# GNN layer on one core: transposing transfers in place of TensorE's transposes of h

## Chip, cores and metric

One core of a Trainium2 chip runs the whole layer. The metric is the device time of one execution in microseconds (us). The kernel before took 1001.66 us (median of three runs, 1001.43 to 1001.74).

## What is computed

x is 8192 x 256 (fp32), adj is 8192 x 8192 (int32, 0 or 1). Cut to what matters:

```
h    = relu(layernorm(x))                        # rows of x, eps 1e-5
self = h @ W_self + b_self
agg  = (adj > 0) @ h / max(degree, 1)
nb   = agg @ W_nb + b_nb
out  = x + relu(concat(self, nb) @ W_comb + b_comb)
```

## The kernel before

The weights are multiplied together first, so that one product of h with 512 columns gives a self part (256 columns, kept in fp32 as `self_f`) and a part z (256 columns) that the adjacency then sums. The kernel has two stages.

The **projection stage** makes z and the self part. The 8192 rows are 64 tiles of 128 rows, taken in 32 pairs (`PAIRS`), and x comes in 16 chunks (`CHUNKS`) of four tiles, 512 KB each, so a chunk is two pairs. For each pair j the engines do this:

- VectorE (`dve`): `stats_of(j)` (lines 432 to 442), the mean and variance of its rows, two BATCH_NORM_STATS2 and two aggregates.
- GpSimd (`pool`, lines 251 to 260): once for each chunk, four small instructions turn mean and variance into a scale and a shift. They wait until VectorE has aggregated all four tiles of the chunk (line 252).
- ScalarE (`act`): `norm(j)` (line 264) writes h = relu(scale x + shift) over x in `self_f`.
- TensorE (`pe`): `turn(j)` (line 326), four fp32 transposes into one bank of PSUM (`turn_ps`).
- ScalarE: `high_of_h(j)` (line 272) copies the turned h to fp16. VectorE: `low_of_h(j)` (line 444) subtracts that copy from the turned h and writes the remainder as fp16. High and low half of h stand in a ring of three slots (`h_t`, RING = 3).
- TensorE: `project(j)` (line 339), 12 matmuls of 512 columns into a pair of banks (`pair_ps`, a ring of three): for each of two tiles and two halves of the inner dimension, high times high, high times low and low times high.
- ScalarE: `copy_self(j)` and `high_of_z(j)` empty the bank, VectorE: `low_of_z(j)` writes the low half of z.

Each engine's order is written out by hand. On VectorE step j of the loop at line 514 is low_of_h(j + 1), low_of_z(j - 2), stats_of(j + 6), and in the four steps of `MASK_STEPS` one mask of the first adjacency tile (`form_mask`, `turn_mask`). On TensorE it is turn(j + 2), project(j). SyncE (`sp`) issues every transfer: first all 16 chunks of x with the first adjacency tile's four groups (1 MB each) between them, then tiles 1 and 2 of the adjacency, one group at a time as mask buffers come free (`load_tile`, line 182).

The **summing stage** goes over 64 tiles of the adjacency's rows: VectorE makes a 0/1 mask and transposes it in blocks, ScalarE counts it, TensorE multiplies it with z in 64 matmuls (`sum_chunk`, line 355), and VectorE finishes the tile. `tile(0, 0)` on TensorE begins as soon as the last projection is out.

Of the kernel before, what the change touches and what calls it, by code (L numbers as in the profile page):

```python
# [5 lines left out]
F32 = mybir.dt.float32  # L6
# [35 lines left out]
RING = 3  # L42

MASK_STEPS = (5, 11, 17, 23)

# [3 lines left out]
def graph_layer(nc, x, adj, w_self_t, w_nb_t, w_comb, b_cols_in, b_comb, out):  # L49
# [6 lines left out]
    with ExitStack() as ctx:  # L56
# [3 lines left out]
        def sem(name):  # L60
            return ctx.enter_context(nc.semaphore(name))
# [23 lines left out]
        PAIR = 2 * 2 * HALVES * P  # L85
        h_t = spare[:, 0:RING * PAIR].rearrange("p (n i t h m) -> p n i t h m", n=RING, i=2, t=2, h=HALVES)
        w12 = spare[:, RING * PAIR:RING * PAIR + 4 * HALVES * D].rearrange("p (i h n) -> p i h n", i=2, h=HALVES)

# [31 lines left out]

        turn_ps = [ctx.enter_context(nc.psum_tensor(f"turn_ps{n}", [P, 2 * D], F32)) for n in range(2)]
        pair_ps = [ctx.enter_context(nc.psum_tensor(f"pair_ps{n}", [P, 2, 2 * D], F32)) for n in range(RING)]

        acc = [pair_ps[2][:, 0, :], pair_ps[2][:, 1, :], pair_ps[0][:, 0, :], pair_ps[0][:, 1, :]]
        deg_ps = [turn_ps[0][:, 0:1], turn_ps[1][:, 0:1], pair_ps[1][:, 0, 0:1], pair_ps[1][:, 1, 0:1]]

# [20 lines left out]
        normed = sem("normed")  # L147
        h_turned = sem("h_turned")
        h_high = sem("h_high")
# [25 lines left out]
        def _(sp):  # L175
# [11 lines left out]
            def store(r):  # L187
                sp.wait_ge(out_ready, r + 1)
                sp.dma_start(out[r, :, :], x_again[:, r % XRING, :]).then_inc(stored, DONE)

            load_x(0)
            for n, (dst, w) in enumerate(((ws_t, w_self_t), (wn_t, w_nb_t))):
# [6 lines left out]
            sp.dma_start(bc_row, b_comb.rearrange("(a n) -> a n", a=1).partition_broadcast(P)).then_inc(b_loaded, DONE)  # L199
            for e in range(2, 6):  # L200
                load_x(e)
            for a in range(QUAD):
                load_group(0, a)
                load_x(6 + a)
            for e in range(6 + QUAD, CHUNKS):
                load_x(e)
            for r in range(1, 3):
# [33 lines left out]
        @block.gpsimd  # L241
        def _(pool):
            pool.memset(ident, 0.0).then_inc(zeroed, 1)
            pool.memset(power, -0.5).then_inc(zeroed, 1)
            pool.memset(ones, 1.0).then_inc(zeroed, 1)
            pool.memset(eight[:, :], SUM_HELD).then_inc(zeroed, 1)
            pool.wait_ge(zeroed, 4)
            pool.affine_select(out=ident, in_=ident, compare_op=ALU.not_equal, fill=1.0, base=0,
                               pattern=[[-1, P]], channel_multiplier=1).then_inc(ident_ready, 1)

            for e in range(CHUNKS):
                pool.wait_ge(aggr_done, SUB * (e + 1))
                pool.tensor_scalar(var_s[:, e % 2, :], mean_var[:, e, :, 1], EPS, H_SCALE ** -2,
                                   ALU.add, ALU.mult).then_inc(var_ready, 1)
                pool.tensor_scalar(minus_mean[:, e % 2, :], mean_var[:, e, :, 0], -1.0, None, ALU.mult).then_inc(negated, 1)
                pool.wait_ge(var_ready, e + 1)
                pool.tensor_tensor(rstd[:, e, :], var_s[:, e % 2, :], power, ALU.pow).then_inc(rstd_ready, 1)
                pool.wait_ge(rstd_ready, e + 1)
                pool.wait_ge(negated, e + 1)
                pool.tensor_tensor(shift[:, e, :], minus_mean[:, e % 2, :], rstd[:, e, :], ALU.mult).then_inc(shift_ready, 1)  # L260

        @block.scalar
        def _(act):
# [7 lines left out]

            def high_of_h(j):
                act.wait_ge(h_turned, j + 1)
                if j >= RING:
                    act.wait_ge(projected, j - RING + 1)
                act.activation(h_t[:, j % RING, 0, :, :, :].rearrange("p t h m -> p (t h m)"), turn_ps[j % 2][:, :],  # L276
                               ACT.Copy).then_inc(h_high, 1)

            def high_of_z(j):
                act.activation(z16[:, 2 * j:2 * j + 2, 0:D], pair_ps[j % RING][:, :, D:2 * D], ACT.Copy, scale=Z_SCALE  # L280
                               ).then_inc(z_high, 1)

            def copy_self(j):
                act.wait_ge(projected, j + 1)
                act.activation(self_f[:, 2 * j:2 * j + 2, :], pair_ps[j % RING][:, :, 0:D], ACT.Copy, scale=SELF_SCALE  # L285
                               ).then_inc(self_copied, 1)
# [8 lines left out]
            for n in range(2):  # L295
# [3 lines left out]
                               ).then_inc(w_high, 1)  # L299
            high_of_h(0)  # L300
            norm(2)

            for j in range(PAIRS + 1):
                if j + 1 < PAIRS:
                    high_of_h(j + 1)
                if j + 3 < PAIRS:
                    norm(j + 3)
                if j >= 1:
                    copy_self(j - 1)
                    high_of_z(j - 1)  # L310
                for a, at in enumerate(COUNT_STEPS):
                    if at == j:
                        count(0, 0, a)
# [11 lines left out]
        def _(pe):  # L325
            def turn(j):
                pe.wait_ge(normed, 2 * (j + 1))
                if j >= 2:
                    pe.wait_ge(h_low, j - 1)
                for t in range(2):  # L330
                    for half in range(HALVES):
                        at = (t * HALVES + half) * P
                        mm = pe.transpose(turn_ps[j % 2][:, at:at + P], self_f[:, 2 * j + t, half * P:(half + 1) * P],  # L333
                                          ident)
                mm.then_inc(h_turned, 1)

            TERMS = ((0, 0), (0, 1), (1, 0))

            def project(j):
                pe.wait_ge(h_low, j + 1)  # L340
                if j == 0:
                    pe.wait_ge(w_ready, 2)
                if j >= RING:
                    pe.wait_ge(z_low, j - RING + 1)
                    pe.wait_ge(self_copied, j - RING + 1)
                if j == 2:
                    pe.wait_ge(c_ready, 1)
                for t in range(2):
                    steps = [(half, i, w) for half in range(HALVES) for i, w in TERMS]
                    for at, (half, i, w) in enumerate(steps):  # L350
                        mm = pe.matmul(pair_ps[j % RING][:, t, :], h_t[:, j % RING, i, t, half, :], w12[:, w, half, :],  # L351
                                       start=(at == 0), stop=(at == len(steps) - 1))
                mm.then_inc(projected, 1)
# [14 lines left out]

            pe.wait_ge(ident_ready, 1)
            for n, w_t in enumerate((ws_t, wn_t)):  # L370
# [5 lines left out]
                mm.then_inc(w_product, 1)  # L376
            turn(0)
            turn(1)
            pe.wait_ge(wide_ready, 2 * HALVES)
# [4 lines left out]
            for j in range(PAIRS):  # L384
                if j + 2 < PAIRS:
                    turn(j + 2)
                project(j)
# [30 lines left out]
        def _(dve):  # L418
# [25 lines left out]
            def low_of_h(j):  # L444
                flat = "p t h m -> p (t h m)"
                dve.wait_ge(h_high, j + 1)
                dve.scalar_tensor_tensor(h_t[:, j % RING, 1, :, :, :].rearrange(flat), turn_ps[j % 2][:, :], 1.0,  # L447
                                         h_t[:, j % RING, 0, :, :, :].rearrange(flat), ALU.mult, ALU.subtract
                                         ).then_inc(h_low, 1)

            def low_of_z(j):
                dve.wait_ge(z_high, j + 1)
                dve.scalar_tensor_tensor(z16[:, 2 * j:2 * j + 2, D:2 * D], pair_ps[j % RING][:, :, D:2 * D], Z_SCALE,  # L453
                                         z16[:, 2 * j:2 * j + 2, 0:D], ALU.mult, ALU.subtract).then_inc(z_low, 1)
# [52 lines left out]
            w_low(1)  # L507
            low_of_h(0)
            for p in range(4, 6):
                stats_of(p)  # L510
# [3 lines left out]
            for j in range(PAIRS + 2):  # L514
                if j + 1 < PAIRS:
                    low_of_h(j + 1)
                if j >= 2:
                    low_of_z(j - 2)
                if j + 6 < PAIRS:
                    stats_of(j + 6)  # L520
                if j in MASK_STEPS:
                    a = MASK_STEPS.index(j)
                    form_mask(0, a, first=True)
                    turn_mask(0, 0, a)
# [69 lines left out]
```

## Time and profile before

| | |
|---|---|
| median of three runs | 1001.66 us |
| the profiled execution | 1001.76 us, of which its span is 1000.0 us |
| projection stage, TensorE (first projection to first sum) | 14.96 to 110.50 us of the span |
| summing stage, TensorE | 110.50 us to 996.3 us |
| granted clock of TensorE over the span | 1.0 |

The span runs from the first to the last instruction in the trace; the rest of the execution's time (1.76 us) lies around it. In the rows below an instruction is named by its engine and its line in the kernel (L351 is line 351), by what it writes and reads, and by its shape. PE is TensorE's matmuls, PEld its weight loads, DVE is VectorE, ACT ScalarE, POOL GpSimd, SP SyncE. A tensor that lies inside another bears the other's name: h_t and the product of the weights lie in `mask_t`, the statistics in `x_again`, h and x in `self_f`.

### The profile page before, as it was taken

How to read it: one execution, taken by the hardware profiler on the slowest of the kernel's cores; microseconds unless marked ns; L12 is line 12 of the kernel's file. 1: busy time of each engine (PE TensorE's matmuls, PEld its weight loads, DVE VectorE, ACT ScalarE, POOL GpSimd, SP SyncE). 2: the span in 40 equal slices, each digit the busy share in tenths (PEclk: the TensorE clock that was granted, in tenths of full speed). 3: DMA queues.
4: the chain of work that ended last, by engine and by line, in shares of the span. 5: the costliest groups of instructions: out<-in, count | busy, mean ns of one | idle time of the engine just before them, and what ended most of it. 6: DMA issues, size and time to landing. Idle time of an engine off the chain costs nothing.

```text
span 1000.0 us, 14269 instructions
## 1 busy us (share of the span) xinstructions
PE 989.9 (99%) x4696; PEld 460.5 (46%) x4696; DVE 673.9 (67%) x1163; ACT 585.0 (59%) x675; POOL 30.5 (3%) x73
## 2 busy tenths in 40 slices
PE   7999999999999999999999999999999999999998
PEld 4555444444444444444444444444444444444443
DVE  6886677986776666766667666676666766667711
ACT  5888886775655556655556555565555655556500
POOL 2332000000000000000000000000000000000000
PEclk9999999999999999999999999999999999999999
DMA  9621399999888898888988888888888888888600
GB/s 344 251 85 43 140 421 371 416 420 377 320 316 321 312 341 317 319 322 312 342 312 322 322 313 336 318 322 322 312 328 328 323 315 321 321 326 326 218 16 10
DMA packets 58994, 295.04 MB, mean 295 GB/s; under 512 B 6624, under 2 KB 24160, under 8 KB 26208
## 3 DMA queue, kind: packets, MB, share of 16 engines
q1 hardware_dynamic: 58976, 294.81, 78.6%
q8 instruction: 10, 0.16, 0.1%
q14 instruction: 8, 0.07, 0.0%
HBM read 286.39 MB, written 8.39 MB: 295 GB/s over the span
## 4 chain that ended last, share of the span: by engine, by line
PE 98%; DMA 1%; DVE 0%; SPq 0%; issue 0%
PE pair_ps L360 89%; PE pair_ps L351 8%; PE turn_ps L333 1%; DMA self_f<-in_x_dram 1%; PE pair_ps L381 0%; DVE x_again L439 0%; SPq L195 0%; SPq L193 0%; DVE z L505 0%; DVE fold L502 0%; DVE x_again L442 0%; DVE part L485 0%; DVE part L482 0%; DVE x_again L488 0%; SPq L177 0%
## 5 line engine op out<-in xcount | busy, mean ns | idle before, releaser
L360 PE MATMUL pair_ps<-z,mask_t 128*128 128x512 f16 x4096 | 885.8, 379 | 0.0
L290 ACT ACTIVATE mask<-mask 128x2048 uint8<-128x2048 uint8 x256 | 488.0, 1908 | 341.4 <-DVE mask_t L430 341.4
L360 PEld LDWEIGHTS pair_ps<-z,mask_t 128*128 128x128 fp8e4 x4096 | 396.2, 98 | 475.7
L430 DVE STREAM_TRANSPOSE mask_t<-mask 128x512 uint32<-128x512 uint32 x256 | 181.7, 710 | 219.8 <-PE pair_ps L360 214.3
L424 DVE TENSOR_SCALAR mask<-stage 128x2048 uint8<-128x2048 int32 x256 | 308.1, 1203 | 6.0 <-DMA stage<-in_adj_dram 5.9
L351 PE MATMUL pair_ps<-mask_t 128*128 128x512 f16 x384 | 87.8, 379 | 0.0
L351 PEld LDWEIGHTS pair_ps<-mask_t 128*128 128x128 f16 x384 | 37.6, 98 | 38.6
L290 ACT ACTIVATION_READ_ACCUMULATOR mask<-mask 128x1 f32 x256 | 48.1, 188 | 0.0
L482 DVE SCALAR_TENSOR_TENSOR part<-pair_ps,rdeg,self_f 128x256 f32<-128x256 f32 x64 | 31.0, 484 | 15.7 <-DVE rdeg L477 11.9
L269 ACT ACTIVATE self_f<-self_f,x_again 128x256 f32<-128x256 f32 x64 | 35.0, 605 | 8.7 <-POOL x_again L260 8.7
L447 DVE SCALAR_TENSOR_TENSOR mask_t<-turn_ps,mask_t 128x512 f16<-128x512 f32 x32 | 21.8, 681 | 19.3 <-ACT mask_t L276 19.3
L485 DVE SCALAR_TENSOR_TENSOR part<-pair_ps,rdeg,part 128x256 f32<-128x256 f32 x64 | 31.0, 484 | 2.3
L488 DVE SCALAR_TENSOR_TENSOR x_again<-part,x_again 128x256 f32<-128x256 f32 x64 | 27.2, 425 | 2.2
L439 DVE BATCH_NORM_STATS2 x_again<-self_f 128x6 f32<-128x256 f32 x64 | 23.7, 411 | 7.3 <-DMA self_f<-in_x_dram 7.3
L285 ACT ACTIVATE self_f<-pair_ps 128x512 f32<-128x512 f32 x32 | 19.1, 597 | 14.8 <-PE pair_ps L351 14.8
L453 DVE SCALAR_TENSOR_TENSOR z<-pair_ps,z 128x512 f16<-128x512 f32 x32 | 21.8, 681 | 5.6 <-ACT z L280 5.6
L470 DVE TENSOR_TENSOR self_f<-self_f,c_row 128x256 f32 (+1 forms) x64 | 24.5, 383 | 0.0
L276 ACT ACTIVATE mask_t<-turn_ps 128x512 f16<-128x512 f32 x32 | 19.3, 603 | 0.0
L461 DVE SCALAR_TENSOR_TENSOR spread<-deg_part,fold 128x128 f16<-128x128 f32 x64 | 18.0, 281 | 1.8 <-ACT mask L290 1.8
L333 PE MATMUL turn_ps<-x_again,self_f 128*128 128x128 f32 x128 | 19.1, 273 | 0.0
L280 ACT ACTIVATE z<-pair_ps 128x512 f16<-128x512 f32 x32 | 19.0, 594 | 0.0
L333 PEld LDWEIGHTS turn_ps<-x_again,self_f 128*128 128x128 f32 x128 | 15.9, 141 | 6.0 <-ACT self_f L269 0.3
(31 smaller groups left out, 93.0 us busy)
## 6 DMA issues: line engine op xcount, KB each, us to landing
stage<-in_adj_dram SPq DMA_DIRECT2D x256, 1024.0 KB, 5.9
self_f<-in_x_dram SPq DMA_DIRECT2D x16, 512.0 KB, 15.4
x_again<-in_x_dram SPq DMA_DIRECT2D x64, 128.0 KB, 5.3
out_dram<-x_again SPq DMA_DIRECT2D x64, 128.0 KB, 5.1
z<-in_L_gnn_W_comb_dram SPq DMA_DIRECT2D x2, 256.0 KB, 4.8
z<-in_L_gnn_W_self_dram SPq DMA_DIRECT2D x1, 256.0 KB, 3.6
z<-in_L_gnn_W_nb_dram SPq DMA_DIRECT2D x1, 256.0 KB, 4.5
z<-in_L_gnn_b_comb_dram SPq DMA_DIRECT2D x1, 128.0 KB, 6.4
```

What stands on the lines that cost most here:

```text
L269: act.activation(t, t, ACT.Relu, bias=shift[:, e, s:s + 1], scale=rstd[:, e, s:s + 1]).then_inc(normed, 1)
L290: act.activation(mask[:, a, :], mask[:, a, :], ACT.Copy, accum_out=deg_part[:, n, a:a + 1]).then_inc(counted, 1)
L333: mm = pe.transpose(turn_ps[j % 2][:, at:at + P], self_f[:, 2 * j + t, half * P:(half + 1) * P], ident)
L351: mm = pe.matmul(pair_ps[j % RING][:, t, :], h_t[:, j % RING, i, t, half, :], w12[:, w, half, :], start=(at == 0), stop=(at == len(steps) ...
L360: mm = pe.matmul(acc[n], bytes_of[:, :, s], z16[:, SUB * e + s, :], start=(e == 0 and s == 0), stop=(e == CHUNKS - 1 and s == SUB - 1))
L424: dve.tensor_scalar(mask[:, a, :], stage[:, a, :], 0.0, float(ONE_BYTE), ALU.is_gt, ALU.mult).then_inc(masked, 1)
L430: dve.transpose(mask_t[:, n, :, a, :], src).then_inc(transposed, 1)
L439: dve.bn_stats(stats[:, e % 2, s, :], self_f[:, SUB * e + s, :]).then_inc(stats_done, 1)
L470: dve.tensor_tensor(own_of(r), own_of(r), c_row[:, :], ALU.add).then_inc(biased, 1)
L482: dve.scalar_tensor_tensor(part[:, :], acc[n][:, D:2 * D], rdeg[:, n:n + 1], own, ALU.mult, ALU.add).then_inc(low_added, 1)
L485: dve.scalar_tensor_tensor(part[:, :], acc[n][:, 0:D], rdeg[:, n:n + 1], part[:, :], ALU.mult, ALU.add).then_inc(sum_read, 1)
L488: dve.scalar_tensor_tensor(x_again[:, n, :], part[:, :], 0.0, x_again[:, n, :], ALU.max, ALU.add).then_inc(out_ready, 1)
```

## The change

- h is no longer turned by TensorE. GpSimd casts h (`self_f`, rows as they are) to fp16, `high_of_h(j)`, one instruction of 128 x 512 for each pair; VectorE's `low_of_h(j)` subtracts it from h, both read from SBUF; both halves go to a new ring `h16` of three slots. SyncE then issues two transposing transfers for each pair (`turn(j)`, one for each tile, 128 rows x 512 columns of fp16, from `h16` to `h_t`), and `project(j)` waits for these.
- ScalarE's `high_of_h` and TensorE's `turn` are gone, and so are the two banks `turn_ps`: `pair_ps` has four pairs of banks (`BANKS`) in place of three.
- GpSimd's work for a chunk becomes `rstd_of(e)` and its order is: chunks 0 and 1, then for each pair j the cast, and after every odd pair the chunk (j + 3) / 2.
- VectorE's loop does low_of_h(j + 2) at step j, ScalarE's does norm(j + 4).
- SyncE issues chunks 0 to 3 of x at the start, and then, pair by pair, one chunk at every even pair (chunk j / 2 + 4), one group of the first adjacency tile at pairs 1, 7, 13 and 19, and `turn(j)`, which waits for low_of_h(j) and, from pair 3 on, for project(j - 3). Tiles 1 and 2 of the adjacency follow after turn(31).

The diff, cut to its core:

```diff
+BANKS = 4
+
+LOAD_STEPS = (1, 7, 13, 19)
 MASK_STEPS = (5, 11, 17, 23)
...
+        h16 = spare[:, 0:RING * PAIR].rearrange("p (n t i d) -> p n t i d", n=RING, t=2, i=2)
+        h_t = spare[:, RING * PAIR:W_AT].rearrange("p (n t i h m) -> p n t i h m", n=RING, t=2, i=2, h=HALVES)
...
+            def turn(j):
+                sp.wait_ge(h_low, j + 1)
+                if j >= RING:
+                    sp.wait_ge(projected, j - RING + 1)
+                    sp.wait_ge(h_turned[j % RING], 2 * (j // RING) * DONE)
+                for t in range(2):
+                    sp.dma_start_transpose(h_t[:, j % RING, t, :, :, :].rearrange("p i h m -> p (i h) m"),
+                                           h16[:, j % RING, t, :, :].rearrange("p i d -> p (i d)")
+                                           ).then_inc(h_turned[j % RING], DONE)
...
-            for e in range(2, 6):
-                load_x(e)
-            for a in range(QUAD):
-                load_group(0, a)
-                load_x(6 + a)
-            for e in range(6 + QUAD, CHUNKS):
-                load_x(e)
+            load_x(2)
+            load_x(3)
+            for j in range(PAIRS):
+                e = j // 2 + 4
+                if j % 2 == 0 and e < CHUNKS:
+                    load_x(e)
+                if j in LOAD_STEPS:
+                    load_group(0, LOAD_STEPS.index(j))
+                turn(j)
             for r in range(1, 3):
                 load_tile(r)
...
-            for e in range(CHUNKS):
+            def rstd_of(e):
                 pool.wait_ge(aggr_done, SUB * (e + 1))
...
+            def high_of_h(j):
+                pool.wait_ge(normed, 2 * (j + 1))
+                if j >= RING:
+                    pool.wait_ge(h_turned[j % RING], 2 * (j // RING) * DONE)
+                pool.tensor_copy(h16[:, j % RING, :, 0, :], self_f[:, 2 * j:2 * j + 2, :]).then_inc(h_high, 1)
+
+
+            rstd_of(0)
+            rstd_of(1)
+            for j in range(PAIRS):
+                high_of_h(j)
+                if j % 2 and (j + 3) // 2 < CHUNKS:
+                    rstd_of((j + 3) // 2)
...
             def project(j):
-                pe.wait_ge(h_low, j + 1)
+                pe.wait_ge(h_turned[j % RING], 2 * (j // RING + 1) * DONE)
...
-                if j >= RING:
-                    pe.wait_ge(z_low, j - RING + 1)
-                    pe.wait_ge(self_copied, j - RING + 1)
+                if j >= BANKS:
+                    pe.wait_ge(z_low, j - BANKS + 1)
+                    pe.wait_ge(self_copied, j - BANKS + 1)
...
             for j in range(PAIRS):
-                if j + 2 < PAIRS:
-                    turn(j + 2)
                 project(j)
...
             def low_of_h(j):
-                flat = "p t h m -> p (t h m)"
                 dve.wait_ge(h_high, j + 1)
-                dve.scalar_tensor_tensor(h_t[:, j % RING, 1, :, :, :].rearrange(flat), turn_ps[j % 2][:, :], 1.0,
-                                         h_t[:, j % RING, 0, :, :, :].rearrange(flat), ALU.mult, ALU.subtract
-                                         ).then_inc(h_low, 1)
+                dve.scalar_tensor_tensor(h16[:, j % RING, :, 1, :], self_f[:, 2 * j:2 * j + 2, :], 1.0,
+                                         h16[:, j % RING, :, 0, :], ALU.mult, ALU.subtract).then_inc(h_low, 1)
...
             low_of_h(0)
+            low_of_h(1)
             for p in range(4, 6):
                 stats_of(p)
...
             for j in range(PAIRS + 2):
-                if j + 1 < PAIRS:
-                    low_of_h(j + 1)
+                if j + 2 < PAIRS:
+                    low_of_h(j + 2)
                 if j >= 2:
                     low_of_z(j - 2)
                 if j + 6 < PAIRS:
                     stats_of(j + 6)
```

## Rows read from the trace of the kernel before

**Rows 1.** The page: busy time by engine, and the last-ending chain by line.

```profile
PE 989.9 (99%) x4696; PEld 460.5 (46%) x4696; DVE 673.9 (67%) x1163; ACT 585.0 (59%) x675; POOL 30.5 (3%) x73
...
PE pair_ps L360 89%; PE pair_ps L351 8%; PE turn_ps L333 1%; DMA self_f<-in_x_dram 1%; PE pair_ps L381 0%; DVE x_again L439 0%; SPq L195 0%; SPq L193 0%; DVE z L505 0%; DVE fold L502 0%; DVE x_again L442 0%; DVE part L485 0%; DVE part L482 0%; DVE x_again L488 0%; SPq L177 0%
```

**Rows 2.** Both stages: busy us (instructions) by engine; last: clock, DMA share, GB/s.

```profile
14.85:110.29 95.44, 95.44 (x503) 51.17 (x502) 71.47 (x182) 78.68 (x153) 26.32 (x56) 1.00 0.37 144
110.29:996.00 885.71, 885.71 (x4162) 402.42 (x4160) 593.71 (x950) 499.71 (x512) 0.00 (x0) 1.00 0.83 313
```

**Rows 3.** Timeline: start and duration in us; [idle before, releaser]. Projection's first and last.

```profile
14.96 2.75 PE L351 MATMUL pair_ps<-mask_t 128*128 128x512 f16 x12
...
110.50 38.15 PE L360 MATMUL pair_ps<-z,mask_t 128*128 128x512 f16 x176
```

**Rows 4.** Timeline, one step of a pair: TensorE and VectorE.

```profile
32.45 0.66 DVE L447 SCALAR_TENSOR_TENSOR mask_t<-turn_ps,mask_t 128x512 f16<-128x512 f32 x1
...
32.68 0.60 PE L333 MATMUL turn_ps<-x_again,self_f 128*128 128x128 f32 x4
...
33.02 0.68 DVE L453 SCALAR_TENSOR_TENSOR z<-pair_ps,z 128x512 f16<-128x512 f32 x1
33.12 2.75 PE L351 MATMUL pair_ps<-mask_t 128*128 128x512 f16 x12
...
33.62 0.73 DVE L439 BATCH_NORM_STATS2 x_again<-self_f 128x6 f32<-128x256 f32 x2
...
34.39 0.25 DVE L442 BATCH_NORM_AGGREGATE x_again<-x_again 128x2 f32<-128x6 f32 x2
34.55 0.66 DVE L447 SCALAR_TENSOR_TENSOR mask_t<-turn_ps,mask_t 128x512 f16<-128x512 f32 x1
...
35.71 0.60 PE L333 MATMUL turn_ps<-x_again,self_f 128*128 128x128 f32 x4
```

**Rows 5.** Timeline, GpSimd's work for one chunk, and what released it.

```profile
25.10 0.25 DVE L442 BATCH_NORM_AGGREGATE x_again<-x_again 128x2 f32<-128x6 f32 x2
...
25.44 0.19 POOL L253 TENSOR_SCALAR x_again<-x_again 128x4 f32<-128x4 f32 x1 [3.99 <-DVE x_again L442]
...
27.02 0.20 POOL L260 TENSOR_TENSOR x_again<-x_again 128x4 f32<-128x4 f32 x1
```

**Rows 6.** Timeline, GpSimd's larger instructions at the start.

```profile
0.73 0.20 POOL L243 MEMSET x_again<- 128x128 f32 x1 [0.29 <-POOLq L572]
...
0.87 0.10 POOL L244 MEMSET x_again<- 128x4 f32 x1
...
1.38 0.29 POOL L248 TENSOR_SCALAR_AFFINE_SELECT x_again<-x_again 128x128 f32<-128x128 f32 x1 [0.24 <-POOL eight L246]
```

**Rows 7.** The page's groups: VectorE's three-input forms, count, busy us, mean ns.

```profile
L482 DVE SCALAR_TENSOR_TENSOR part<-pair_ps,rdeg,self_f 128x256 f32<-128x256 f32 x64 | 31.0, 484 | 15.7 <-DVE rdeg L477 11.9
...
L488 DVE SCALAR_TENSOR_TENSOR x_again<-part,x_again 128x256 f32<-128x256 f32 x64 | 27.2, 425 | 2.2
```

**Rows 8.** Timeline, a mask on VectorE and GpSimd's instruction beside it.

```profile
30.58 1.19 DVE L424 TENSOR_SCALAR mask<-stage 128x2048 uint8<-128x2048 int32 x1
30.75 1.07 POOL L253 TENSOR_SCALAR x_again<-x_again 128x4 f32<-128x4 f32 x1 [3.53 <-DVE x_again L442]
```

**Rows 9.** Timeline around chunk 1: GpSimd's last instruction, and VectorE's weights.

```profile
12.46 1.28 DVE L493 SCALAR_TENSOR_TENSOR mask_t<-pair_ps,mask_t 128x512 f16<-128x512 f32 x2
...
12.93 0.20 POOL L260 TENSOR_TENSOR x_again<-x_again 128x4 f32<-128x4 f32 x1
```

**Rows 10.** SyncE's issue of one transfer (timeline), and x's landing times (tile view).

```profile
10.66 0.44 SPq L177 DMA_DIRECT2D self_f<-in_x_dram  x1
...
DMA to landing us min/median/max: 3.4/15.4/21.2
```

**Rows 11.** Timeline, the second adjacency tile's first mask.

```profile
113.30 1.22 DVE L424 TENSOR_SCALAR mask<-stage 128x2048 uint8<-128x2048 int32 x1
```

More of the change, by code:

```diff
@@ L85, in graph_layer @@
         PAIR = 2 * 2 * HALVES * P
-        h_t = spare[:, 0:RING * PAIR].rearrange("p (n i t h m) -> p n i t h m", n=RING, i=2, t=2, h=HALVES)
-        w12 = spare[:, RING * PAIR:RING * PAIR + 4 * HALVES * D].rearrange("p (i h n) -> p i h n", i=2, h=HALVES)
+        W_AT = 2 * RING * PAIR
+        h16 = spare[:, 0:RING * PAIR].rearrange("p (n t i d) -> p n t i d", n=RING, t=2, i=2)
+        h_t = spare[:, RING * PAIR:W_AT].rearrange("p (n t i h m) -> p n t i h m", n=RING, t=2, i=2, h=HALVES)
+        w12 = spare[:, W_AT:W_AT + 4 * HALVES * D].rearrange("p (i h n) -> p i h n", i=2, h=HALVES)
         late = z16[:, 3 * TILES // 4:, :].rearrange("p t n -> p (t n)").bitcast(F32)
@@ L119, in graph_layer @@
         power = small(SUB)
[L121 to L125, printed above, removed]
+        pair_ps = [ctx.enter_context(nc.psum_tensor(f"pair_ps{n}", [P, 2, 2 * D], F32)) for n in range(BANKS)]
+        acc = [pair_ps[0][:, 0, :], pair_ps[0][:, 1, :], pair_ps[1][:, 0, :], pair_ps[1][:, 1, :]]
+        deg_ps = [pair_ps[2][:, 0, 0:1], pair_ps[2][:, 1, 0:1], pair_ps[3][:, 0, 0:1], pair_ps[3][:, 1, 0:1]]
         w_loaded = [sem(f"w_loaded{n}") for n in range(2)]
@@ L147, in graph_layer @@
         normed = sem("normed")
-        h_turned = sem("h_turned")
+        h_turned = [sem(f"h_turned{n}") for n in range(RING)]
         h_high = sem("h_high")
@@ L270, in norm @@
                                    ).then_inc(normed, 1)
-            def high_of_h(j):
-                act.wait_ge(h_turned, j + 1)
-                if j >= RING:
-                    act.wait_ge(projected, j - RING + 1)
-                act.activation(h_t[:, j % RING, 0, :, :, :].rearrange("p t h m -> p (t h m)"), turn_ps[j % 2][:, :],
-                               ACT.Copy).then_inc(h_high, 1)
             def high_of_z(j):
-                act.activation(z16[:, 2 * j:2 * j + 2, 0:D], pair_ps[j % RING][:, :, D:2 * D], ACT.Copy, scale=Z_SCALE
+                act.activation(z16[:, 2 * j:2 * j + 2, 0:D], pair_ps[j % BANKS][:, :, D:2 * D], ACT.Copy, scale=Z_SCALE
                                ).then_inc(z_high, 1)
@@ L284, in copy_self @@
                 act.wait_ge(projected, j + 1)
-                act.activation(self_f[:, 2 * j:2 * j + 2, :], pair_ps[j % RING][:, :, 0:D], ACT.Copy, scale=SELF_SCALE
+                act.activation(self_f[:, 2 * j:2 * j + 2, :], pair_ps[j % BANKS][:, :, 0:D], ACT.Copy, scale=SELF_SCALE
                                ).then_inc(self_copied, 1)
@@ L299, in _ @@
                                ).then_inc(w_high, 1)
-            high_of_h(0)
             norm(2)
+            norm(3)
             for j in range(PAIRS + 1):
-                if j + 1 < PAIRS:
-                    high_of_h(j + 1)
-                if j + 3 < PAIRS:
-                    norm(j + 3)
+                if j + 4 < PAIRS:
+                    norm(j + 4)
                 if j >= 1:
@@ L325, in _ @@
         def _(pe):
[L326 to L335, printed above, removed]
             TERMS = ((0, 0), (0, 1), (1, 0))
             def project(j):
-                pe.wait_ge(h_low, j + 1)
+                pe.wait_ge(h_turned[j % RING], 2 * (j // RING + 1) * DONE)
                 if j == 0:
                     pe.wait_ge(w_ready, 2)
-                if j >= RING:
-                    pe.wait_ge(z_low, j - RING + 1)
-                    pe.wait_ge(self_copied, j - RING + 1)
+                if j >= BANKS:
+                    pe.wait_ge(z_low, j - BANKS + 1)
+                    pe.wait_ge(self_copied, j - BANKS + 1)
                 if j == 2:
@@ L350, in project @@
                     for at, (half, i, w) in enumerate(steps):
-                        mm = pe.matmul(pair_ps[j % RING][:, t, :], h_t[:, j % RING, i, t, half, :], w12[:, w, half, :],
+                        mm = pe.matmul(pair_ps[j % BANKS][:, t, :], h_t[:, j % RING, t, i, half, :], w12[:, w, half, :],
                                        start=(at == 0), stop=(at == len(steps) - 1))
@@ L367, in sum_degrees @@
                           start=True, stop=True).then_inc(deg_summed, 1)
-            pe.wait_ge(ident_ready, 1)
             for n, w_t in enumerate((ws_t, wn_t)):
@@ L376, in _ @@
                 mm.then_inc(w_product, 1)
-            turn(0)
-            turn(1)
             pe.wait_ge(wide_ready, 2 * HALVES)
@@ L444, in low_of_h @@
             def low_of_h(j):
-                flat = "p t h m -> p (t h m)"
                 dve.wait_ge(h_high, j + 1)
-                dve.scalar_tensor_tensor(h_t[:, j % RING, 1, :, :, :].rearrange(flat), turn_ps[j % 2][:, :], 1.0,
-                                         h_t[:, j % RING, 0, :, :, :].rearrange(flat), ALU.mult, ALU.subtract
-                                         ).then_inc(h_low, 1)
+                dve.scalar_tensor_tensor(h16[:, j % RING, :, 1, :], self_f[:, 2 * j:2 * j + 2, :], 1.0,
+                                         h16[:, j % RING, :, 0, :], ALU.mult, ALU.subtract).then_inc(h_low, 1)
             def low_of_z(j):
                 dve.wait_ge(z_high, j + 1)
-                dve.scalar_tensor_tensor(z16[:, 2 * j:2 * j + 2, D:2 * D], pair_ps[j % RING][:, :, D:2 * D], Z_SCALE,
+                dve.scalar_tensor_tensor(z16[:, 2 * j:2 * j + 2, D:2 * D], pair_ps[j % BANKS][:, :, D:2 * D], Z_SCALE,
                                          z16[:, 2 * j:2 * j + 2, 0:D], ALU.mult, ALU.subtract).then_inc(z_low, 1)
@@ L514, in _ @@
             for j in range(PAIRS + 2):
-                if j + 1 < PAIRS:
-                    low_of_h(j + 1)
+                if j + 2 < PAIRS:
+                    low_of_h(j + 2)
                 if j >= 2:
```

## The prediction

> **What bounds the kernel now.** I read the profile's page first. TensorE is busy 99% of the span and the chain that ended last is nearly all TensorE: sums 89%, projections 8%, transposes 1% [rows 1]. So time is won only by TensorE doing less before its last sum, and lost by any gap opened in it. The view by stretches then splits the span [rows 2]: 95.44 us of projection stage and 885.7 us of summing stage, TensorE without a gap in both, clock 1.00. The change touches the first alone. The sums have 13.84 us a tile (885.7 / 64), and their first instruction comes at 110.50 [rows 3]: whatever moves that moment moves the end by as much.
>
> The timeline of one pair shows what that stage costs [rows 4]. From one transpose group to the next are 35.71 - 32.68 = 3.03 us: 0.44 for the transposes (32.68 to 33.12) and 2.59 for the 12 matmuls (33.12 to 35.71). VectorE's step of low_of_h, low_of_z and statistics is 34.55 - 32.45 = 2.10 us, so it has slack. GpSimd works 1.78 us for a chunk (25.44 to 27.22) and otherwise waits, always for VectorE's aggregates [rows 5].
>
> **The change, part by part.** *Removed from TensorE:* 30 of the 32 transpose groups lie in the stretch, 30 x 0.44 = 13.2 us, all on the path. Kept fed, TensorE would need 32 x 2.59 = 82.9 us.
>
> *GpSimd's order.* This decides, in my reading of the code. The work for chunk (j + 3) / 2 stands behind the cast of odd pair j and waits for the statistics of pair j + 4. VectorE takes these in step j - 2, behind low_of_h(j), which waits for that very cast. And the cast of pair j + 1 stands behind the chunk's work on GpSimd, while VectorE's next instruction, low_of_h(j + 1), waits for it. So the two engines take turns, once for every chunk (two pairs). One round, from rows:
> - aggregate to GpSimd: 25.35 to 25.44, 0.09;
> - the chunk's four instructions, 1.78;
> - the cast of the even pair: c;
> - back to VectorE: 0.09, taken alike;
> - VectorE's step of the even pair: 2.10 (the odd pair's cast runs beside it);
> - VectorE's step of the odd pair to the end of its aggregates: 32.45 to 34.64, 2.19.
>
> Together 6.25 + c.
>
> *The cast c* (512 elements, fp32 to fp16) is not in the trace. GpSimd's memsets take 0.10 for 4 elements and 0.20 for 128 [rows 6]; 0.83 ns an element gives 0.10 + 508 x 0.00083 = 0.53, the low end, since a memset reads nothing. The select takes 0.29 for 128; on the same base that is 1.5 ns an element and 0.89 us, and four times 0.29 is 1.17, the high end. I take 0.89, since the select reads and writes as a cast does. The round is then **7.14 us, 3.57 a pair, against 3.03 before**.
>
> *low_of_h* now reads h from SBUF. The same form from PSUM takes 484 ns and from SBUF 425 for 256 columns [rows 7]; I leave it at its 0.66, and count 0.06 a piece, 0.12 a round, for the low end. At the high end it is blocked (rival 1).
>
> *Masks.* In four steps a mask follows the statistics, and GpSimd's first instruction beside it took 1.07 in place of 0.19 [rows 5, 8]. That is off the path now and on it then: 4 x 0.88 = 3.5. The mask itself (30.58 to 32.45, where low_of_h starts [rows 4, 8]) is hidden behind GpSimd's 1.78 + 0.88 + c.
>
> *The start.* GpSimd finishes chunk 1 at 13.13 and VectorE the weights at 13.74 [rows 9]; the casts of pairs 0 and 1 end at 14.91. low_of_h(1) and two steps of statistics (0.09 + 0.57 + 0.93 + 1.02) bring the last aggregate to 17.52. The first round has no low_of_z (2 x 0.60 less): 17.61 + 5.94 = 23.55. Twelve rounds of 7.14 follow: 109.2, with the masks 112.7. There chunk 15 begins; 1.78 + 0.89 + 0.09 + 0.66 later low_of_h(28) is done: 116.1.
>
> *The transfers.* Two a pair, issued by SyncE. A transposing transfer is not in the trace. An issue takes 0.44, and the quickest chunk of x (four times the bytes) landed 3.4 us after its issue [rows 10]: 0.44 + 3.4 = 3.8 from low_of_h to project. Pair 28 starts at 119.9. From there TensorE is fed, since a transfer may take the 5.2 us that two projections last. The low end is a quarter of 3.4, 3 us less; the high end is two landings one after the other, 7.2 a pair (rival 2).
>
> *End:* 119.9 + 4 x 2.59 = 130.3, against 110.50: **+19.8 us**. On the execution's own 1001.76 that is 1021.6; the median lies 0.10 below it, which I neglect. I give 1022.
>
> *Costed at nothing.* ScalarE loses 32 casts, but it is no bound: 78.68 busy of 95.44 [rows 2]. The fourth pair of banks lets TensorE run further ahead, of no use to one that starves. The chunks of x, moved between the steps, are issued eight pairs before their rows are turned, some 28 us. If this cover is gone VectorE's statistics wait for x and the round is longer by that. SyncE's issues are 0.88 a pair, 0.22 for x, four groups, all below 3.57. Tile 1's adjacency, issued so far as its stage buffers came free, now stands behind turn(31), which waits for project(28): at about 123.4 it is issued; the first group lands 3.4 later, at the 313 GB/s of the summing stage [rows 2] a megabyte takes 3.3, so the fourth lands near 137 and its mask stands near 139, due by 130.3 + 13.84 = 144. Before, VectorE formed the first of these masks 2.8 us after the sums began [rows 3, 11]; it is hidden with some 5 us to spare.
>
> **The rivals.** *1. The cast holds VectorE up.* GpSimd goes straight from the even pair's cast to the odd pair's, just when low_of_h of the even pair should start. That a GpSimd instruction can be held through one of VectorE's is in the rows: the 1.07 above ended at 31.82, with the mask that ended at 31.77 [rows 8]. If low_of_h waits for the odd cast in this way, the round grows by c: 14 times 0.89, +12.5, **1034**. Against: that row has a mask, not this form, and GpSimd as the one that waits; were low_of_h first, the cast would wait, which costs nothing. The Trainium skill (SBUF — State Buffer, "Who interferes with whom") says that a VectorE instruction with two SBUF inputs and a GpSimd instruction that reads SBUF exclude each other, the first to start holding the ports to its end. By that, low_of_h as it is now written comes under the rule, and the sum would be 1034 where the cast starts first and 1022 where it does not.
>
> *2. The transfers bound.* Over 3.57 a pair the queue decides in place of the round, each 0.1 us adding 3.2. Nothing in the trace tells a transposing transfer's pace; between 0.88 and 7.2 a pair lies 3.57, and at 4.5 the stage ends near 14.9 + 32 x 4.5 + 4 = 163, **1054**. Against: 3.4 is mostly delay, which overlaps from transfer to transfer. The Trainium skill (VectorE: DVE Perf Modes, "The three transpose paths") gives 1309 ns for a 128 x 128 block by DMA. Eight such blocks a pair, if they ran one by one, would be an estimated 10.5 us and a time near 1240; no row here bears on it.
>
> *3. TensorE stays fed, and the change wins.* Place: the round. It decides at two pairs of the old pace: were the round about 5.7 us or less, 14 times 1.4 would take the 19.8 back. At 5.2 (2 x 2.59) TensorE is the bound: first projection at 14.0 + 0.7 + 3.8 = 18.5, end 18.5 + 82.9 = 101.4, 9.1 earlier, **993**. For: TensorE loses 0.44 a pair. Against: with c at its low end the round is still 6.78, and 6.25 with no cast at all; only a chunk's work shorter than its 1.78, which no edit shortens, would do it.
>
> *4. No change:* a round near 5.7, needing the same and a chance meeting.
>
> **How the numbers follow.** Chances: forecast 0.52, cast holding VectorE 0.27, transfers 0.13, faster 0.05, no change 0.03. A measurement of this kernel can tell 0.2%, 2 us, from no change. Slower is 0.52 + 0.27 + 0.13 = 0.92. Range: the low end of the cast, 16 casts x 0.36 = 5.8 less, and low_of_h's 1.6 less, give 1014, and a quicker landing a little under: 1013. The high end, 16 x 0.28 = 4.5 more, gives 1026, and rival 1 with it 1034 to 1042; I stop at 1038. Left out are most of rival 2 and rivals 3 and 4, about 2 in 10.
>
> **What would show it.** In the changed kernel's trace the first sum should begin near 130, not 110. TensorE should have gaps in the projection stage, about 2 us in every two pairs, ended by the transfers. GpSimd's L253 should wait for VectorE's aggregate once per chunk, and VectorE's low_of_h of even pairs for GpSimd's cast, for some 2.7 us; the starts of GpSimd's chunk work should stand 7.1 us apart. Cast: 0.53 to 1.17. If low_of_h of even pairs starts only when the odd cast ends, or lasts 1.5 us, rival 1 holds. If SyncE's issues stand end to end, or VectorE has long waited when transfers land, rival 2. The forecast is wrong if chunk starts follow TensorE's pace (5.2 or 6.1 apart), or if a wait for x or adjacency opens gaps in the summing stage.

## The result, and the profile after

The changed kernel takes **1022.4 us** (median of 4 runs) against 1001.7: a ratio of 1.0205, 95% interval 1.019 to 1.022. The forecast was 1022, range 1013 to 1038. Ratios here and below compare the executions that agree with one another; two of the ten of experiment 9, at 2694.69 and 3710.02 us, are left out of its ratio, and no trace shows what made them slow.

Lines of the page after: busy time, the chain that ended last by line, and three groups that answer to [rows 1, 5, 7].

```profile
PE 984.6 (96%) x4568; PEld 445.9 (44%) x4568; DVE 679.0 (67%) x1163; ACT 569.1 (56%) x643; POOL 48.4 (5%) x105
...
PE pair_ps L370 87%; DVE x_again L444 2%; PE pair_ps L361 2%; DVE z L456 1%; DVE mask_t L451 1%; POOL mask_t L282 1%; DVE x_again L447 1%; PE pair_ps L383 1%; POOL x_again L269 1%; DMA z<-in_L_gnn_W_comb_dram 0%; DMA mask_t<-mask_t 0%; POOL x_again L271 0%; POOL x_again L276 0%; SPq L201 0%; POOL x_again L273 0%
...
L451 DVE SCALAR_TENSOR_TENSOR mask_t<-self_f,mask_t 128x512 f16<-128x512 f32 x32 | 26.8, 839 | 30.8 <-POOL mask_t L282 30.8
...
L282 POOL CAST mask_t<-self_f 128x512 f16<-128x512 f32 x32 | 18.8, 611 | 5.0 <-DMA mask_t<-mask_t 5.0
...
mask_t<-mask_t SPq DMA_TRANSPOSE x64, 2.6
```

TensorE is busy 5 us less, yet its share falls to 96%: the chain no longer runs through its projections (8% before, 2% now) but through VectorE and GpSimd. The stretches of the two stages (columns as in [rows 2]) place the loss.

```profile
18.67:130.20 111.53, 89.78 (x381) 36.93 (x382) 73.69 (x173) 61.91 (x121) 41.86 (x84) 0.95 0.70 169
130.20:1016.10 885.90, 885.90 (x4163) 402.46 (x4162) 594.39 (x951) 500.69 (x512) 0.00 (x0) 1.00 0.84 316
```

The first stretch, which ends 0.84 us before the first sum, has 22 us of gaps in TensorE's work (111.53 less 89.78 busy); before there were none. The timeline has the first sum at 131.04, against 110.50 in [rows 3]: 20.5 us later, which is all of the 20.5 by which the span grew. From the first sum to the end of the span it is 889.5 us in both (1020.5 less 131.04, 1000.0 less 110.50): the summing stage is what it was.

```profile
131.04 4.26 PE L370 MATMUL pair_ps<-z,mask_t 128*128 128x512 f16 x19
```

One round of GpSimd and VectorE, from the timeline after (start and duration in us):

```profile
52.24 0.25 DVE L447 BATCH_NORM_AGGREGATE x_again<-x_again 128x2 f32<-128x6 f32 x2
52.58 0.20 POOL L269 TENSOR_SCALAR x_again<-x_again 128x4 f32<-128x4 f32 x1 [4.29 <-DVE x_again L447]
...
54.31 1.17 POOL L282 CAST mask_t<-self_f 128x512 f16<-128x512 f32 x2
...
54.95 1.07 DVE L451 SCALAR_TENSOR_TENSOR mask_t<-self_f,mask_t 128x512 f16<-128x512 f32 x1 [2.46 <-POOL mask_t L282]
...
57.48 0.66 DVE L451 SCALAR_TENSOR_TENSOR mask_t<-self_f,mask_t 128x512 f16<-128x512 f32 x1
...
59.44 0.25 DVE L447 BATCH_NORM_AGGREGATE x_again<-x_again 128x2 f32<-128x6 f32 x2
...
59.77 1.07 POOL L269 TENSOR_SCALAR x_again<-x_again 128x4 f32<-128x4 f32 x1 [4.29 <-DVE x_again L447]
...
67.84 0.19 POOL L269 TENSOR_SCALAR x_again<-x_again 128x4 f32<-128x4 f32 x1 [4.29 <-DVE x_again L447]
```

GpSimd stands 4.29 us until VectorE's aggregates, VectorE 2.46 us until GpSimd's cast: each waits while the other works. From 52.58 to 59.77 are 7.19 us for two pairs. Where a mask falls in (59.77, 1.07 in place of 0.20) the round that begins there is 0.88 longer (67.84 - 59.77 = 8.07). The two casts take 0.61 each, and low_of_h of the even pair 1.07, where that of the odd pair takes 0.66.

SyncE's transposing transfers in the whole changed kernel, by line: issue in ns and landing in us (from the start of the issue to the arrival of the data), each as least, median and most; behind the issue the starts of the first and the last.

```profile
L201 SPq DMA_TRANSPOSE mask_t<-mask_t x64: 1188/1267/2398, 14.8 to 125.3; - x64
...
DMA to landing us min/median/max: 2.4/2.6/5.9
```

### The profile page after: what moved, and what is told of

Its sections match the earlier page's. It is cut to its first block, busy times and chain, and to the rows that moved or that the text cites. A ratio compares the mean times of both kernels' runs of the same rounds, so it can differ in the third digit from the quotient of the medians.

```text
span 1020.5 us, 14074 instructions
## 1 busy us (share of the span) xinstructions
PE 984.6 (96%) x4568; PEld 445.9 (44%) x4568; DVE 679.0 (67%) x1163; ACT 569.1 (56%) x643; POOL 48.4 (5%) x105
## 4 chain that ended last, share of the span: by engine, by line
PE 89%; DVE 5%; issue 3%; POOL 2%; DMA 1%; SPq 0%; ACT 0%; POOLq 0%
PE pair_ps L370 87%; DVE x_again L444 2%; PE pair_ps L361 2%; DVE z L456 1%; DVE mask_t L451 1%; POOL mask_t L282 1%; DVE x_again L447 1%; PE pair_ps L383 1%; POOL x_again L269 1%; DMA z<-in_L_gnn_W_comb_dram 0%; DMA mask_t<-mask_t 0%; POOL x_again L271 0%; POOL x_again L276 0%; SPq L201 0%; POOL x_again L273 0%
## 5 line engine op out<-in xcount | busy, mean ns | idle before, releaser
L361 PE MATMUL pair_ps<-mask_t 128*128 128x512 f16 x384 | 90.8, 395 | 25.9 <-DMA mask_t<-mask_t 25.8
L451 DVE SCALAR_TENSOR_TENSOR mask_t<-self_f,mask_t 128x512 f16<-128x512 f32 x32 | 26.8, 839 | 30.8 <-POOL mask_t L282 30.8
L478 DVE TENSOR_SCALAR deg<-pair_ps 128x1 f32<-128x1 f32 x64 | 7.9, 123 | 37.5 <-PE pair_ps L376 37.5
L282 POOL CAST mask_t<-self_f 128x512 f16<-128x512 f32 x32 | 18.8, 611 | 5.0 <-DMA mask_t<-mask_t 5.0
L273 POOL TENSOR_TENSOR x_again<-x_again 128x4 f32<-128x4 f32 x16 | 16.6, 1037 | 0.0
```

The source lines that it names most:

```text
L282: pool.tensor_copy(h16[:, j % RING, :, 0, :], self_f[:, 2 * j:2 * j + 2, :]).then_inc(h_high, 1)
L361: mm = pe.matmul(pair_ps[j % BANKS][:, t, :], h_t[:, j % RING, t, i, half, :], w12[:, w, half, :], start=(at == 0), stop=(at == len(steps) ...
L451: dve.scalar_tensor_tensor(h16[:, j % RING, :, 1, :], self_f[:, 2 * j:2 * j + 2, :], 1.0, h16[:, j % RING, :, 0, :], ALU.mult, ALU.subtrac ...
```

## The experiments

All are the changed kernel with the edits named. Each result is the median in us, then in brackets its ratio to the kernel before, with the 95% interval; the kernel before ran beside them at medians of 1001.8 to 1002.5. The time rows come from one execution, which need not be the median one.

**1. The order on GpSimd alone.**

```diff
-                if j % 2 and (j + 3) // 2 < CHUNKS:
-                    rstd_of((j + 3) // 2)
+                if j % 2 == 0 and j >= 2 and (j + 2) // 2 < CHUNKS:
+                    rstd_of((j + 2) // 2)
```

> The changed kernel with one line of GpSimd's order changed: a chunk's four instructions stand behind the cast of an even pair j (chunk (j + 2) / 2) and no longer behind the odd pair before it, so that VectorE's step of the even pair runs beside them. By the theory that the turn-taking of GpSimd and VectorE set the pace (rounds of 7.19 us for two pairs), the round falls to about 4.7 us, SyncE's issues (2 x 1.27 + 0.29 a pair, 2.9) become the bound, the first sum comes near 111 in place of 131, and the time is 1000 to 1006 us. By the rival that the transposing transfers set the pace already, nothing moves: 1020 to 1023.

Measured 1012.2 us (ratio 1.010, 1.008 to 1.012). One moved line gives back half of the loss, so the round held the changed kernel; but 1012 is neither number. SyncE's timeline shows a candidate for the next bound, in two pairs, a chunk of x and the next two pairs:

```profile
61.81 5.28 SPq L201 DMA_TRANSPOSE mask_t<-mask_t  x4
67.13 0.58 SPq L181 DMA_DIRECT2D self_f<-in_x_dram  x1
67.82 5.57 SPq L201 DMA_TRANSPOSE mask_t<-mask_t  x4
```

SyncE issues end to end: 67.82 - 61.81 = 6.0 us for two pairs, 3.0 a pair, as slow as the old kernel's 3.03. The expectation of 2.9 left out the gaps between issues. The start came late too: the first projection begins at 19.93, 5.0 later than the 14.96 of the kernel before, and from there to the first sum at 120.12 are 100.2 us, 3.13 a pair on average. That SyncE's issues alone set this pace is not shown: GpSimd's casts also wait 19.8 us for transfers, and experiment 4 takes issues away and gains nothing.

**2. The odd cast held back**, so that nothing on GpSimd runs beside low_of_h of the even pair.

```diff
                 pool.wait_ge(normed, 2 * (j + 1))
+                if j % 2:
+                    pool.wait_ge(h_low, j)
```

> The changed kernel with one wait added: GpSimd's cast of an odd pair waits until low_of_h of the even pair before it is done. By the theory that this cast holds low_of_h up (1.07 us where it stands beside the cast, 0.66 elsewhere), low_of_h of even pairs falls to 0.66, the round from 7.19 to about 6.75, and the time by 13 x 0.43, to 1016 to 1018 us. By the rival that low_of_h of even pairs is slow for a reason of its own, its 1.07 stays, and the time is 1022 or more.

Measured 1018.6 (1.016, 1.014 to 1.018). In the view by line low_of_h is 656 to 693 ns for all 32, none at 1.07, and two chunk starts stand 51.67 - 44.84 = 6.83 apart:

```profile
44.84 0.19 POOL L269 TENSOR_SCALAR x_again<-x_again 128x4 f32<-128x4 f32 x1 [3.02 <-DVE x_again L449]
...
51.67 0.20 POOL L269 TENSOR_SCALAR x_again<-x_again 128x4 f32<-128x4 f32 x1 [3.02 <-DVE x_again L449]
```

So the cast did hold low_of_h up: without it the round is 0.36 us shorter. The time fell too, though by less than expected (1018.6 lies 0.6 above the range); the rival expectation falls.

**3. x issued by ScalarE, order as changed.** Chunks 4 and 5 at the start, 6 to 15 from ScalarE's loop.

```diff
+                if j % 2 == 0 and j // 2 + 6 < CHUNKS:
+                    e = j // 2 + 6
+                    act.dma_start(chunk_of(self_f, e)..., x[e, :, :]).then_inc(x_full[e], DONE)
```

> The changed kernel with chunks 6 to 15 of x issued by ScalarE and chunks 4 and 5 at the start, so that only the transposing transfers and four adjacency groups are left between the steps on SyncE. By the theory of the round nothing moves: 1021 to 1024 us. By the rival that SyncE's queue sets the pace, the 10 issues of 0.58 us taken out of it bring some 6 us: 1016 or less.

Measured 1023.4 (1.0215, 1.020 to 1.023). Nothing moved, as the round has it: SyncE's queue did not set the changed kernel's pace.

**4. Both 1 and 3.**

> Both: the order of e1_order and x issued by ScalarE. By the theory of the round SyncE is then left with 2 x 1.27 us a pair, about as much as TensorE's 2.59, and the first sum comes near 18.7 + 32 x 2.6 + 1 = 103: 992 to 997 us, below the kernel before. By the rival that transposing transfers bound at over 2.9 us a pair whatever is issued beside them, it stays where e1_order is.

Measured 1014.8 (1.012, 1.009 to 1.015): a miss, no better than 1, as the rival had it. The view by line has SyncE's transfers land after 2.4 to 8.4 us, median 3.5 (2.6 in the changed kernel), and GpSimd's cast waits for a transfer 16 times, 33.0 us in all.

```profile
POOL mask_t L279 <- DMA mask_t<-mask_t: 33.0, 16, 5.2
...
DMA to landing us min/median/max: 2.4/3.5/8.4
```

Unloading SyncE was worth nothing here: with a ring of three slots the cast must wait when a transfer lands late.

**5. As 4, rings of five slots** (`RING = 5`, the spare space one slot of `mask_t` earlier).

> As e4_order_xact (GpSimd's order mended, x issued by ScalarE) with rings of five slots in place of three for both halves of h. Theory: with the round gone, what was left in e4_order_xact (1015) is the time from a freed slot to a landed transfer, up to 8.4 us when a load of x or adjacency is under way, against 5.2 us that two projections cover; five slots cover four projections, 10.4 us, so TensorE is fed: first sum near 104, 994 to 999 us. Rival: the transfers' own pace beside loads is the bound, more slots only move the wait, and the time stays over 1008 us.

Measured 1011.1 (1.008, 1.007 to 1.010). The cast's waits for transfers are gone, yet TensorE still waits for them, 16.8 us in 6 waits; landing is up to 10.0 us. The time is on the rival's side. Whether the slots brought anything is open, since the intervals of 4 and 5 overlap.

```profile
PE pair_ps L361 <- DMA mask_t<-mask_t: 16.8, 6, 5.1
```

**6. One transposing transfer a pair**, 128 x 1024, order as changed.

```diff
-                for t in range(2):
-                    sp.dma_start_transpose(h_t[:, j % RING, t, ...
+                sp.dma_start_transpose(h_t[:, j % RING, ...].rearrange("p t i h m -> p (t i h) m"),
+                                       h16[:, j % RING, ...].rearrange("p t i d -> p (t i d)"))
```

The counts that wait for a pair's transfers are halved with it.

> The changed kernel with one transposing transfer of 128 x 1024 for each pair in place of two of 128 x 512; all else as changed. By the theory of the round the time stays: 1020 to 1023 us. By the rival that SyncE's issue of two transfers a pair sets the pace it falls by what the issue loses. The issue itself: if its 1.27 us is a fixed part near the 0.43 of an ordinary issue and the rest goes with the columns, one of 1024 takes some 2.1 us; if it is all columns, 2.5.

Measured 1022.7 (1.020, 1.018 to 1.022): again the round holds. The issue was expected to grow with the columns and does not: 1.23 us for 1024 columns, 1.27 for 512 (medians, view by line); landing 3.1 for 2.6.

```profile
L200 SPq DMA_TRANSPOSE mask_t<-mask_t x32: 1231/1232/1871, 15.9 to 124.8; - x32
```

**7. Order, five slots, one transfer a pair**, x with SyncE.

> The changed kernel with GpSimd's order mended (as e1_order), rings of five slots, and one transposing transfer for each pair; x stays with SyncE between the steps. Theory: SyncE's work a pair falls from about 3.07 to 2.1 + 0.29 + 0.1 = 2.5, just under TensorE's 2.59, and five slots cover the landing: first sum near 105, 994 to 1000 us, below the kernel before. Rival: the pace of the transposing transfers beside loads, not their issue, held e1_order at 1012: then over 1006 us.

Measured 1006.0 (1.0035, 1.002 to 1.005): at the edge of the rival's side. SyncE now has gaps, so its issues no longer set the pace, and the cast no longer waits for a slot. The timeline shows another round:

```profile
48.70 0.54 POOL L268 TENSOR_SCALAR x_again<-x_again 128x4 f32<-128x4 f32 x1 [2.04 <-DVE x_again L446]
...
50.86 1.09 ACT L298 ACTIVATE self_f<-self_f,x_again 128x256 f32<-128x256 f32 x2 [1.98 <-POOL x_again L275]
...
52.34 0.58 ACT L302 ACTIVATE z<-pair_ps 128x512 f16<-128x512 f32 x1
...
52.95 0.69 DVE L455 SCALAR_TENSOR_TENSOR z<-pair_ps,z 128x512 f16<-128x512 f32 x1 [0.85 <-ACT z L302]
...
54.34 0.25 DVE L446 BATCH_NORM_AGGREGATE x_again<-x_again 128x2 f32<-128x6 f32 x2
...
54.68 1.07 POOL L268 TENSOR_SCALAR x_again<-x_again 128x4 f32<-128x4 f32 x1 [2.04 <-DVE x_again L446]
```

Chunk's work, norm, high_of_z behind it, low_of_z, the statistics behind that, the next chunk's work: 54.68 - 48.70 = 5.98. Experiments 8 and 9 cut this round in two ways.

**8. As 7, statistics ahead of low_of_z** in VectorE's step.

```diff
-                if j >= 2:
-                    low_of_z(j - 2)
                 if j + 6 < PAIRS:
                     stats_of(j + 6)
+                if j >= 2:
+                    low_of_z(j - 2)
```

> As e7_order_ring_merge, but VectorE takes the statistics before low_of_z in each step. Theory: what held e7_order_ring_merge at 6.0 us for two pairs is a second, longer round: chunk's work on GpSimd, norm on ScalarE, the copies behind it, low_of_z, the statistics behind that, the next chunk's work. With the statistics ahead of low_of_z that chain is cut, the pace falls toward TensorE's 5.2, and the time to 996 to 1001 us. Rival: the landing of transfers beside loads (3.6 us, up to 6.9) holds it: 1005 to 1008.

Measured **997.9** (0.9961, 0.9946 to 0.9975), below both kernels and in the expected range. TensorE waits for transfers 4.0 us in all, 3.40 of it ahead of the first projection, and the first sum comes at 104.67:

```profile
17.89 8.15 PE L360 MATMUL pair_ps<-mask_t 128*128 128x512 f16 x24 [3.40 <-DMA mask_t<-mask_t]
26.20 44.36 PE L360 MATMUL pair_ps<-mask_t 128*128 128x512 f16 x204 [0.16 <-DMA mask_t<-mask_t]
71.00 33.84 PE L360 MATMUL pair_ps<-mask_t 128*128 128x512 f16 x156 [0.43 <-DMA mask_t<-mask_t]
104.67 20.67 PE L369 MATMUL pair_ps<-z,mask_t 128*128 128x512 f16 x95
```

Of the 13.2 us taken from TensorE this execution (995.95, the fastest of its five) keeps 5.8: 104.67 against 110.50. The first projection starts 2.9 later than before (17.89 for 14.96). The first two pairs then take 8.15 us, where two take 5.35 in the changed kernel at 46.65: behind its wait of 3.40 TensorE's granted clock is 0.50 from 17.8 to 22.0, the lower level of 1.2 GHz, and 1.00 from 24.0 on.

**9. As 7, statistics eight pairs ahead** (`stats_of(j + 8)`, pairs 4 to 7 before the loop), and **10. the same with an early start** (casts and low_of_h of pairs 0 and 1 ahead of chunk 1).

> As e7_order_ring_merge, but VectorE takes the statistics eight pairs ahead in place of six, so that GpSimd finds them done. Theory of the two rounds: no engine waits for the chunk's work any more, TensorE is fed at 2.59 a pair, the first sum comes near 17.5 + 83 + 2 = 103, and the time is 992 to 997 us. Rival as before: transfers beside loads, 1005 to 1008.

> As e9_ahead, with the casts of pairs 0 and 1 before chunk 1 on GpSimd and low_of_h(0) and (1) right behind the first four statistics on VectorE, so that the first transfers are issued near 12 in place of 14.4 us. Theory: in a stage that TensorE bounds, the start counts in full, 2 us less than e9_ahead. Rival: the start is covered by a later wait, and the time is that of e9_ahead.

Measured 999.7 (0.9975, 0.996 to 0.999) and 997.6 (0.9949, 0.993 to 0.997). 9 cuts the second round as 8 does, but stops short of its expectation: TensorE waits for transfers 7.4 us, 2.33 of it behind the first projection. 10 against 9 is inconclusive: the intervals overlap, and the first projection is no earlier (17.99, and 17.52 in 9). The trace of 10 can't settle it: it is of one of the slowest of its executions (999.6, of 993.6 to 999.9), in which TensorE's first weights came late (a wait of 8.0 us, 6.1 in 9).

## Why the prediction was right

**The mechanism** was the one named: the turn-taking, at 7.19 us a round where 7.14 was worked out, shown by the rows of the round and by experiments 1, 3 and 6. Its points: low_of_h(28) done at 116.17 (forecast 116.1), first sum at 131.04 (130.3), masks 0.88 each as taken from [rows 8].

**Two terms were mis-sized and nearly cancelled; that the forecast came within 0.4 us is luck.** The cast is 0.61, not 0.89: of the two rows in [rows 6] the memset, at 0.53, was the nearer. And rival 1, given 0.27 beside the forecast, did happen, at half its price, and by neither of the signs that the prediction gave it, a start at the end of the odd cast or 1.5 us: low_of_h of the even pair starts 0.03 us after its cast, with the odd cast under way (54.31 to 55.48 for the two), and ends 0.54 after it, at 56.02. VectorE's step is 57.48 - 54.95 = 2.53 in place of 2.10, 0.43 a round in place of 0.89. The Trainium skill (SBUF — State Buffer, "Who interferes with whom") says that a VectorE instruction with two SBUF inputs contends with a GpSimd instruction that reads SBUF; the trace agrees (1.07 beside the cast, 0.66 without, and experiment 2). With the right cast alone the sum would have been some 4.5 us short; with rival 1 as priced, 12 over. Both lie in the range.

**The transfers** were not the bound here (SyncE stands idle, for one, from 54.61 to 56.05, and experiments 3 and 6 moved nothing), but their price was wrong: an issue was put at 0.44, from [rows 10], and is 1.27. SyncE's share "costed at nothing" is 2 x 1.27 + 0.29 = 2.8 a pair, not 1.1: under 3.6, so hidden, but no longer so in experiment 1, where the issues stand end to end. From low_of_h to project it was 1.27 + 2.6 = 3.9 by the medians, against 3.8: that the landing was put at 3.4 and the issue at 0.44 cancelled too. The 1309 ns a block that the Trainium skill (VectorE: DVE Perf Modes, "The three transpose paths") gives is no pace: a transfer of four such blocks landed in 2.6 us, one of eight in 3.1 (medians).

**A term not counted:** TensorE's clock. After its wait of 3.74 us before 113.80 the granted clock (the third figure from the end) was 0.59 up to 118, so at the lower level, 1.2 GHz, for most of that stretch (weight loads 0.43 us apart), then 1.00.

```profile
113.80:118.00 4.20, 4.20 (x12) 1.58 (x13) 2.90 (x4) 3.03 (x6) 2.36 (x5) 0.59 0.45 92
118.00:131.00 13.00, 13.00 (x62) 5.84 (x60) 5.02 (x8) 8.20 (x13) 0.61 (x1) 1.00 0.57 154
```

That cost little, since the transfers of pair 28 came near 120; the first sum is 0.7 later than forecast, part of which this can be. That share was not tried alone.

## What to carry to other kernels

Before moving work to an idle engine, write down for each in-order engine what stands behind each wait: an engine 5% busy can set the pace when a neighbour's next instruction waits for it and it waits for that neighbour's last one. A step taken off the bound engine is worth its time only if the new supplier keeps up; here 13 us were removed and 20.7 were lost; the 20.7 came back, and 4 of the 13 with them, only after the two rounds were broken, in kernels that also had one transfer a pair and five slots. Whether these two were needed as well was not tried apart.

## What was not expected of the hardware

- A transposing transfer costs SyncE 1.27 us to issue (median, 1.19 at least), two to three times a plain one (0.44 to 0.58), and no more for 1024 columns (1.23) than for 512.
- Transposing transfers landed late in the stretches in which loads of x or adjacency were under way. Those of 512 columns took up to 5.9, 6.1 and 6.2 us with x on SyncE's queue (changed kernel, experiments 1 and 2) and up to 6.4, 8.4 and 10.0 with x on ScalarE's (experiments 3 to 5); those of 1024 columns, all with x on SyncE's, up to 6.2 to 8.5. With the loads of the stage done, the median was 2.5 (512 columns, changed kernel, 109 to 123 us). That the loads are the cause was not tried alone.
- GpSimd's own instructions can lengthen too: in experiment 8 its TENSOR_TENSOR of four elements took 1343 ns on average, 1037 in the changed kernel. Two long ones (1.52 and 1.53 us) had low_of_h and a mask on VectorE beside them; neither was tried alone.
